# A banded self-attention stage: one product for values and softmax sums, reciprocals later, the output projection one unit later

## The reference, cut to the stage that changes

The program is a two-layer decoder: self-attention, cross-attention and a mixture of experts, twice. Only the first self-attention is touched. It has 8 batches of 256 rows, 256 features, 16 heads of 16, and a band: a query sees the keys at most 64 rows away.

## Times and profile before

| | us |
|---|---|
| median of three runs | 1502.38 (1500.22 to 1503.75) |
| the profiled execution | 1504.03 |
| its span in the profile | 1502.4 |
| PE busy in it | 1433.9 (95%) |
| DVE, ACT, POOL busy | 748.7, 619.1, 490.5 |

### The profile page before, as it was taken

One profiled execution on the slowest core, in us unless ns is written; L12 is line 12 of the kernel. 1 busy time (PEld: TensorE's weight loads), 2 busy tenths in 40 slices (PEclk: granted clock), 3 DMA queues, 4 the chain that ended last, 5 costly groups with the idle time before them and its releaser, 6 DMA issues. The chain is left out here.

```text
span 1502.4 us, 34667 instructions
## 1 busy us (share of the span) xinstructions
PE 1433.9 (95%) x11880; PEld 1159.7 (77%) x11881; DVE 748.7 (50%) x2160; ACT 619.1 (41%) x1711; POOL 490.5 (33%) x758
## 2 busy tenths in 40 slices
PE   7999998988999999999999999999899899999998
PEld 5676766767899999976777777777666579999997
DVE  6666757887433333344444444444278862222222
ACT  2433346653222222235445444545366533333332
POOL 3545442444322122223233233333224452222222
PEclk9999999999999999999999999999999999999999
DMA  9920000152243434120000000000001522533332
GB/s 316 333 69 2 2 2 9 45 176 62 50 119 67 144 71 114 32 64 1 0 1 1 1 1 1 1 1 0 1 16 44 174 78 40 149 93 94 94 90 34
DMA packets 79666, 97.46 MB, mean 65 GB/s; under 512 B 10523, under 2 KB 72579, under 8 KB 79555
## 3 DMA queue, kind: packets, MB, share of 16 engines
q1 hardware_dynamic: 64643, 77.58, 16.4%
q0 software_dynamic: 13680, 17.19, 6.6%
q10 hardware_dynamic: 1232, 1.18, 0.2%
HBM read 57.51 MB, written 39.59 MB: 65 GB/s over the span
## 5 line engine op out<-in xcount | busy, mean ns | idle before, releaser
L1741 POOL TENSOR_TENSOR L1a_prob<-L1a_prob,L1a_rtot 128x1024 f32<-128x1024 f32 x64 | 121.1, 1892 | 275.8 <-DVE L1a_rtot L1614 275.8
L2270 PEld LDWEIGHTS L0x_ps<-L0f_rows_t,L0f_w_up 128*128 128x128 f32 x1584 | 183.7, 193 | 10.4 <-issue 9.0
L2270 PE MATMUL L0x_ps<-L0f_rows_t,L0f_w_up 128*128 128x128 f32 x1584 | 185.8, 277 | 5.6 <-issue 4.8
L2346 ACT ACTIVATE L1f_hid<-L1x_ps,L1f_b_up 128x128 f32<-128x128 f32 x296 | 92.4, 363 | 163.0 <-PE L1x_ps L2270 159.7
L2270 PEld LDWEIGHTS L1x_ps<-L1f_rows_t,L1f_w_up 128*128 128x128 f32 x1184 | 139.5, 194 | 3.4 <-issue 1.6
L2270 PE MATMUL L1x_ps<-L1f_rows_t,L1f_w_up 128*128 128x128 f32 x1184 | 140.4, 277 | 0.6 <-ACT L1f_rows_t L2330 0.6
L2279 PE MATMUL L1x_ps<-L1f_w_down,L1f_hid 128*128 128x256 f32 x592 | 134.1, 380 | 1.9 <-issue 1.9
L2214 POOL TENSOR_TENSOR turn<-eps 128x1 f32<-128x1 f32 x74 | 13.6, 184 | 372.3 <-DVE wv L2448 367.7
L1683 ACT ACTIVATE L1a_prob<-L1a_ps_s,L1a_nmax 128x256 f32<-128x256 f32 x256 | 118.2, 473 | 38.1 <-DVE L1a_nmax L1609 38.1
L2279 PEld LDWEIGHTS L1x_ps<-L1f_w_down,L1f_hid 128*128 128x128 f32 x592 | 109.6, 190 | 15.5 <-issue 2.1
L1245 POOL TENSOR_SCALAR_AFFINE_SELECT L0a_prob<-L0a_prob 128x128 f32<-128x128 f32 (+1 forms) x256 | 79.8, 353 | 104.3 <-ACT L0a_prob L1199 104.3
(11 more groups left out here) (486 smaller groups left out, 2812.5 us busy)
## 6 DMA issues: line engine op xcount, KB each, us to landing
expert_table<-zero SPq DMA_DIRECT2D x1, 16640.0 KB, 68.5
L0f_w_up<-in_w_dram SPq DMA_DIRECT2D x8, 1408.0 KB, 6.8
L1f_w_up<-in_w_dram SPq DMA_DIRECT2D x8, 1024.0 KB
L1f_w_down<-in_w_dram SPq DMA_DIRECT2D x8, 1024.0 KB
L0f_w_down<-in_w_dram SPq DMA_DIRECT2D x8, 768.0 KB, 8.7
L1f_rows<-expert_table SPq DMA_DIRECT2D x35, 130.0 KB
L0f_rows<-expert_table SPq DMA_DIRECT2D x32, 130.0 KB
sums<-X SPq DMA_DIRECT2D x8, 256.0 KB
```

Source lines behind the costliest of these rows:

```text
L1741: eng.tensor_tensor(v, v, r.unsqueeze(2).to_broadcast([P, 2 * QT_N, S]), ALU.mult).then_inc(norm_done, 1)
L2270: ins = eng.matmul(ps_h[c][:, o:o + P], w_up[par][:, t, w0:w0 + P], rows_t[:, t, :], start=(t == 0), stop=(t == DT - 1))
L2346: ins = eng.activation(hid[:, c, k * P:(k + 1) * P], ps_h[c][:, k * P:(k + 1) * P], ACT.Gelu, bias=b_up[par][:, 2 * c + k:2 * c + k + 1])
```

```diff
-    MID = [[], [(1, "k")], [(-1, "o")], []]
+    MID = [[], [(1, "k")], [], [(-1, "o")]]
...
+        def weights_of(i, t, head):
+            columns = v_s[i][:, t, :, :].rearrange("p h n -> p (h n)")
+            return columns[:, 2 * DH * head - head % 2:2 * DH * (head + 1) - head % 2]
+        def direct(u):
+            return u >= units - 2
...
                 def sums(b, c):
-                    eng.wait_ge(values_done, 2 * (b * 2 + c + 1))
-                    eng.reciprocal(rsum[:, :], ps_o[:, S:2 * S]).then_inc(rsum_done, 1)
+                    n = b * 2 + c
+                    if n:
+                        eng.wait_ge(o_out, n)
+                    if direct(2 * n):
+                        eng.wait_ge(values_done, 2 * (n + 1))
+                        eng.reciprocal(rsum[:, :], ps_o[:, S:2 * S]).then_inc(rsum_done, 1)
+                    else:
+                        eng.wait_ge(sums_moved, 32 * (n + 1))
+                        eng.reciprocal(rsum[:, :], summed_t[:, :]).then_inc(rsum_done, 1)
...
-                    whole = part(u - 2)[:2] if v == 1 and u > 1 else None
-                    if whole:
-                        sums(*whole)
+                    whole = part(u - 4)[:2] if v == 0 and u >= UNITS else part(u - 2)[:2] if u == units - 1 else None
...
                     shift(u)
-                    if whole:
-                        out(*whole)
                     if u + 1 < units:
                         for r in range(GROUPS):
                             maximum(u + 1, r)
-                    for e in of(MID, u):
+                    if whole:
+                        sums(*whole)
+                        out(*whole)
+                    if u == units - 6:
+                        eng.wait_ge(values_done, u - 1)
+                        eng.memset(v_s[(B - 1) % 2][:, :, HEADS // 2:HEADS, :], 0.0).then_inc(cleared, 1)
+                    for e in of(MID, u) + of(END, u):
                         take(*e)
...
+                def gather(n):
+                    eng.wait_ge(values_done, 2 * (n + 1))
+                    if n:
+                        eng.wait_ge(sums_moved, 32 * n)
+                        eng.wait_ge(values_moved, 32 * n)
+                    eng.activation(both[:, :, :], ps_o[:, :].rearrange("p (w s) -> p w s", w=2), ACT.Copy).then_inc(copied, 1)
+                def move(n):
+                    eng.wait_ge(copied, n + 1)
+                    if n:
+                        eng.wait_ge(o_out, n)
+                    for w in range(2):
+                        eng.dma_start(summed_t[w::2, :], both[1 - w::2, w, :]).then_inc(sums_moved, 16)
+                    for w in range(2):
+                        eng.dma_start(valued_t[w::2, :], both[w::2, w, :]).then_inc(values_moved, 16)
...
+                    if u % 2 == 1 and u > 1:
+                        move(u // 2 - 1)
                     for r in range(GROUPS):
                         exponential(u, r)
+                    if u % 2 == 0 and u:
+                        gather(u // 2 - 1)
...
-                            eng.wait_ge(o_out, u // 2)
-                    for summed in range(2):
+                            eng.wait_ge(copied, u // 2)
+                    for summed in range(2 if direct(u) else 1):
```

More of the change, by code:

```diff
@@ L1005, in attention_banded @@
         rsum, o_t = sb("rsum", [P, S]), sb("o_t", [P, 2, S])
+        both, summed_t, valued_t = sb("both", [P, 2, S]), sb("summed", [P, S]), sb("valued", [P, S])
         built, cleared, tops_cleared = sem("built"), sem("cleared"), sem("tops_cleared")
@@ L1044, in wait_free @@
                 eng.wait_ge(exp_done, u * GROUPS + r + 1)
-        def odd_even(v):
-            return v.rearrange("p (a two) (half d) -> p a (two half) d", two=2, half=2)[:, :, 0::3, :]
+        def weights_of(i, t, head):
[3 more added lines that the diff above has]
+            return u >= units - 2
         with nc.Block() as block:
@@ L1064, in _ @@
                     eng.wait_ge(built, 4 * v + 3)
-                    eng.memset(ones[:, v, v * DH:(v + 1) * DH], 1.0).then_inc(built, 1)
+                    eng.memset(ones[:, v, v::2], 1.0).then_inc(built, 1)
                 eng.memset(none[:, :], 0.0).then_inc(built, 1)
@@ L1095, in take @@
                         ins.then_inc(out_vector, 1)
-                    elif e == "o":
+                    if e == "o":
                         eng.wait_ge(projected, b + 1)
@@ L1116, in sums @@
                 def sums(b, c):
-                    eng.wait_ge(values_done, 2 * (b * 2 + c + 1))
-                    eng.reciprocal(rsum[:, :], ps_o[:, S:2 * S]).then_inc(rsum_done, 1)
+                    n = b * 2 + c
[7 more added lines that the diff above has]
+                        eng.reciprocal(rsum[:, :], summed_t[:, :]).then_inc(rsum_done, 1)
                 def out(b, c):
-                    eng.wait_ge(rsum_done, b * 2 + c + 1)
+                    n = b * 2 + c
+                    eng.wait_ge(rsum_done, n + 1)
                     if c == 0 and b:
                         eng.wait_ge(projected, b)
-                    eng.tensor_tensor(o_t[:, c, :], ps_o[:, 0:S], rsum[:, :], ALU.mult).then_inc(o_out, 1)
+                    if not direct(2 * n):
+                        eng.wait_ge(values_moved, 32 * (n + 1))
+                    eng.tensor_tensor(o_t[:, c, :], ps_o[:, 0:S] if direct(2 * n) else valued_t[:, :], rsum[:, :], ALU.mult).then_inc(o_out, 1)
                 norm(0, 0)
@@ L1130, in _ @@
                 for i in range(2):
-                    eng.memset(v_s[i][:, :, :, :], 0.0).then_inc(cleared, 1)
+                    eng.memset(v_s[i][:, :, :, :], 1.0).then_inc(cleared, 1)
                 norm(1, 0)
@@ L1188, in take @@
                     else:
-                        eng.wait_ge(cleared, 2)
+                        eng.wait_ge(cleared, 3 if b == B - 1 else 2)
                         for t in range(KT):
-                            ins = eng.activation(odd_even(v_s[b % 2][:, t, :, :]), src[:, t, :].rearrange("p (a two d) -> p a two d", two=2, d=DH),
-                                                 ACT.Copy)
+                            ins = eng.activation(v_s[b % 2][:, t, :, 0::2], src[:, t, :].rearrange("p (h d) -> p h d", d=DH), ACT.Copy)
                     ins.then_inc(out_scalar, 1)
@@ L1341, in values @@
                         if u:
-                            eng.wait_ge(o_out, u // 2)
-                    for summed in range(2):
+                            eng.wait_ge(copied, u // 2)
+                    for summed in range(2 if direct(u) else 1):
                         for t in range(KT):
                             for r in range(GROUPS):
-                                o = summed * S + first_key[t]
-                                lhs = ones[:, v, :] if summed else v_s[b % 2][:, t, c * 8 + 2 * r + v, :]
-                                ins = eng.matmul(ps_o[rows(r), o:o + W], lhs, prob[u % 2][:, r, t, :], start=(v == 0 and not summed and t == 0),
-                                                 stop=(v == 1 and t == KT - 1), skip_group_check=True)
+                                o = (summed if direct(u) else v) * S + first_key[t]
+                                lhs = ones[:, v, :] if summed else weights_of(b % 2, t, c * 8 + 2 * r + v)
+                                ins = eng.matmul(ps_o[rows(r), o:o + W], lhs, prob[u % 2][:, r, t, :],
+                                                 start=(t == 0 and (v == 0 and not summed if direct(u) else True)),
+                                                 stop=(t == KT - 1 and (v == 1 or not direct(u))), skip_group_check=True)
                     ins.then_inc(values_done, 1)
@@ L2719, with in_turn @@
     down0[:, 0:full + GATED_TAIL] = i["L0_ffn_W3"].transpose(0, 2, 1)
+    def in_turn(w):
+        return w.reshape(-1, 2, 16, *w.shape[1:]).swapaxes(1, 2).reshape(w.shape)
     laid = {
```

3 lines of the change are left out of this document (2 added, 1 removed).

## The result

The changed kernel has a median of 1494.43 us, against 1502.04 before: ratio 0.9943, interval 0.9921 to 0.9965, so 5 to 12 us faster. One of its four executions took 2434.47 us in a slower state, with a mean granted clock of 0.55; the ratio leaves it out, and the median of the other three is 1493.69. Its profiled execution has a span of 1492.0 us where before's had 1502.4.

A forecast was written before the change was run, and what follows sets the result against it. PE was taken as the bound, busy 170.17 of 173.00 us. First batch −1.7, six batches −9.4, last batch −0.9 and tail +3.2 sum to −8.8, so 1502.4 becomes 1493.6 us; range 1489 to 1499, 63%.

The forecast's parts named there:

- The six batches: Batches from the second on: products with ones removed, less new waits, give −1.57 us each, −9.4 in six.
- The floor: From `turned_scores` to the values of the same unit at least 4.40 us, set by exponentials and band selects.
- The first batch: No "o" there and unit 2 already at its minimum: of 2.68 us removed, −1.7 remains.
- the issues end about 1.5 before it is needed: Ahead of unit 4, ACT's DMA issues finish about 1.5 us before ACT is needed.
- ACT's margin: Ahead of unit 2's exponentials, ACT has 0.65 us to spare with four DMA issues of 0.49 each.
- Rival 2: ACT's issues at 0.9 delay unit 2, about 1501 us (8%), or slow landings hold DVE, 1506 to 1515 (7%).
- The last batch: Unit 2 to unit 3 of the last batch: exponentials about 0.9 us late, gather costs 0.35, −0.9 in all.
- The tail: From `turned_scores` of unit 31 to the last "o": PE waits for the last move's chain, 3.2 us lost.
- Rival 1: More is gained, by a hidden tail wait or a better ring place for "o": 1487 to 1490 us, 8%.
- Rival 3: ACT cannot issue DMAs while SP's fill is queued, blocked to 79 us: 40 us lost, 1533 us, 14%.
- stays short even beside the big fill: Landing of ACT's DMAs to DVE, nearest row 2.1 us for 130 KB, remains short during SP's big fill.
- The barrier argument: Later stages begin behind a barrier, so the stage's −8.8 us carries through to the kernel's time.

The follow-up runs named there:

- half a band: Only one side of the band cut: on the changed kernel 1493.91 us, ratio 0.993; on the kernel before 1505.75 us, ratio 1.0001.
- "o" alone: The kernel before with only the projection "o" moved from unit 3 to unit 4 of a batch: 1514.5 us, ratio 1.006.
- The last run above: Changed kernel with DVE's copies and additions ahead of the reciprocal and the keys' projection moved to unit 3, run again: 1494.08 us, ratio 0.9911.

## Why the prediction came out right, step by step

**The six batches.** Forecast −1.57 each, measured 24.76 to 23.23, −1.53. Two terms inside were off and cancel. Both are 0.16. The wait that went with the move of "o" was taken as the 0.26 of the earlier trace rows; the step from unit 3 to unit 4 grew by 1.40 where "o" adds 1.82, so it was 0.42. The idle column counts only the time in which nothing runs; what the wait costs is seen in the starts. The other: from the values of unit 2 to the next `turned_scores` the forecast had 0.77, and it is 0.93, because the maxima free the bank for it only then. The run with half a band shows that second floor.

**The floor.** The 4.40 from the first batch, taken for every unit, held to 0.01 in unit 2 and unit 4 of each quiet batch. Of 2.68 removed a batch the forecast lost 1.11 again and the kernel 1.15; with the product issued twice the batch got 1.48 longer.

**The first batch.** −1.22 instead of −1.7. Unit 2 lost 0.16 to the maxima, as everywhere. In unit 4 the exponentials came 0.25 late behind the first issues, which beside the fill ended at 40.27:

```profile
38.51 1.76 ACTq L1238 DMA_DIRECT2D L0a_valued<-L0a_both  x2
40.38 1.64 ACT L1219 ACTIVATE L0a_prob<-L0a_ps 128x384 f32<-128x384 f32 x4 [2.50 <-PE L0a_ps L1373]
```

The step that failed is that ahead of unit 4 "the issues end about 1.5 before it is needed": in this one unit the last two issues took 0.88 each, not 0.49. Ahead of unit 4 of the quiet batches it held (108.48 against 110.06). The −0.45 ahead of this batch was not forecast, and nothing in the change accounts for it: before had 29.34, and its variants 28.90 ("o" alone) and 29.98 (half a band), the changed kernel's 28.58 to 29.62. So some 0.5 of the 9.70 is not the change's.

**ACT's margin.** Forecast 0.65 with 0.49 an issue; measured 1.7 with 0.62. Both terms were off. The issue is dearer (a DMA of 64 rows of 1 KB, 0.47 to 0.62). But the working put the issues behind the copies of the queries, and they run beside them: 94.18 against 95.49, 1.3 us won. Rival 2's rule, that it decides at 0.65 an issue, was therefore too near; it would decide near 1.0. Doubled issues crossed it at once, so the mechanism of the rival is real and only its distance was wrong.

**The last batch.** This is the largest miss, −2.14 instead of −1.23 (with the 0.35 for the gather, −0.9), with the same cause. The forecast let the exponentials of unit 30 come 0.9 late behind four issues, and put 0.35 on the gather. The issues ran beside ACT's other work, the exponentials came 0.92 after `turned_scores` at 190.52 (at 191.44, 0.36 behind the last issue, which ended at 191.08), and the wait for `ct` grew from 0.84 to 0.91 only.

**The tail.** Forecast +3.2, measured +3.41. The number is right and the account of it only in part. PE before, then the changed kernel:

```profile
211.47 0.93 PE L1331 MATMUL L0a_ps<-L0a_q_m,L0a_k_m 32*128 32x192 f32 x16 [0.51 <-DVE L0a_q_m L1114]
```

```profile
198.66 1.97 PE L1330 MATMUL L0a_ps<-wo,L0a_o_t 128*128 128x256 f32 x8 [0.81 <-DVE L0a_o_t L1142]
200.55 0.93 PE L1373 MATMUL L0a_ps<-L0a_q_m,L0a_k_m 32*128 32x192 f32 x16
...
205.83 1.13 PE L276 MATMUL L0a_ps<-wo,L0x_bv_wide 128*128 128x256 f32 x4 [0.95 <-DVE X L1108]
```

The chain over the last move is the one described. The last values start at 206.89, which is 11.21 after `turned_scores` of unit 31 at 195.68, forecast 11.0. The reciprocal started 5.65 behind `turned_scores`, not 7.15, and then the product waited 1.49 for the outputs' move, which the forecast had let arrive with the sums: of its two DMAs one landed in 1.9 us and one in 3.9.

But the chain is not what the 3.41 is made of. `turned_scores` of unit 31 to that of unit 32 was 211.47 − 208.79 = 2.68 and is 200.55 − 195.68 = 4.87, 2.19 longer, because the moved "o" of batch 7 now stands between them, with a wait of 0.81 for DVE. From there to the last values it was 5.12 and is 6.34, and only these 1.22 are the chain. Where the last move landed in time or the addition stood ahead of it, the last values came at 9.99 and the tail still lost 2.18. So the forecast's "if it were hidden this would be 0" is wrong: it counted what the moved "o" saves in unit 3 of the last batch and not what it adds in unit 4. The number was met by luck: the reciprocal started 1.5 earlier than forecast, and with a landing of 2 us for the outputs too, the chain would not have shown, as in the kernel with the product issued twice; one landing of 3.9 brought it back. Why that one was late isn't shown. In the repeat of the changed kernel (landing 3.2) the tail lost 2.81. In the whole sum the misses are −0.45 ahead of the first batch, +0.5 in it, −0.25 in the six, −0.9 in the last and +0.2 in the tail, so some of its nearness is that they cancel.

**The rivals.** Rival 1's cause, a hidden tail, didn't come. Rival 3, ACT blocked while SP's fill is in the queues, is refuted by two rows of SP's and ACT's queues in the changed kernel:

```profile
21.95 58.22 SPq L2694 DMA_DIRECT2D wr<-in_wr_dram  x1
...
37.31 0.53 ACTq L1236 DMA_DIRECT2D L0a_summed<-L0a_both  x1
```

SP's issue was held from 21.95 to 80.2; ACT's, in the middle of it, took 0.53, and the longest of all during the fill 1.6. So in this trace ACT's queue is not held with SP's, and what the prediction held possible here, that the two block each other's commands, did not come. The Trainium skill ("DMA: Bandwidth & Descriptors", section "Queues, rings and completion order") gives SP and ACT one ring each on the same 16 DMA engines; the trace agrees with the second part, the shared engines: landings took 5.0 to 6.2 us beside the fill, and 1.9 in the median behind it. So the landing that "stays short even beside the big fill" was three times as long there; it cost nothing, as DVE needs the tiles later. Of its signs of being wrong one came, once: DVE was idle 2.49 for a DMA before L1133, in the tail, where its own sum had it.

**The carry to the end.** The barrier argument held for the profiled execution (−9.67 at the next stage, −10.4 at the end) and for the medians within their interval (−7.6, or −8.35 with the median of 1493.69, with −5 to −12). But it is less exact than these two numbers look: between them the lead was 13.5 (at the expert products behind 396 us of before) and 11.8 (at 720), while both kernels run the same code. The last run above is a warning about it too: the next stage can return several us by its clock.

## What to carry to other kernels

A product that is removed from the bounding engine is worth its time only down to the next chain's floor, and a place in the program where that floor already shows (here the first batch, without "o") gives its size to 0.01. Read waits on a pipelined engine from start to start: the idle column gave 0.26 for 0.42. When a freed engine waits in one unit and is full in the next, move work into the wait (here "k"), and when a move leaves it idle for some us, count the granted clock behind the idle time, not the wait alone. Where an entry moves across the end of a loop, count it on both sides: the move of "o" saved its time in one unit of the last batch and added 2.19 in the next.

## What the runs showed of the hardware

- **The clock.** After 4.58 us without a product TensorE had a granted clock of 0.58 over 88 to 94 us, "o" from 1.89 to 3.75. The same wait filled with 36 records of identity products kept it at 1.00 and gave 2.4 us a batch back.
- **Issues beside copies.** ACT's DMA issues start while its earlier ACTIVATEs run (by 1.3 us here), though later ACTIVATEs wait for them.
- **Two readers of SBUF.** Before, the product read its first operand from PSUM and took 0.42 in all 16 places. In the changed kernel L1142 has both operands in SBUF and runs beside POOL's selects: 0.67 or 0.68 in 11 of 15 places, 0.61 in one and 0.43 in three. POOL's eight took 2.65 to 2.80 there, and 2.46 in units 2 and 4. One place of either kind:

```profile
93.22 0.68 DVE L1142 TENSOR_TENSOR L0a_o_t<-L0a_valued,L0a_rsum 128x256 f32<-128x256 f32 x1
```

```profile
92.97 2.65 POOL L1287 TENSOR_SCALAR_AFFINE_SELECT L0a_prob<-L0a_prob 128x128 f32<-128x128 f32 x8 [1.50 <-ACT L0a_prob L1219]
```

```profile
187.12 0.43 DVE L1142 TENSOR_TENSOR L0a_o_t<-L0a_valued,L0a_rsum 128x256 f32<-128x256 f32 x1
```

  Beside the last one POOL's row is 2.73. With "o" in the third unit the same product ran at 89.85, when POOL had nothing, in 0.42. The Trainium skill ("SBUF — State Buffer", section "SBUF: two separate sides") says that a DVE instruction with two SBUF inputs and a GpSimd instruction that reads SBUF share a pair of ports as an exclusive lock, which the one that starts first has for its whole instruction. The trace agrees where single selects can be told apart: at 93.21 a select started just ahead of the product, which took 0.68; at 46.66 the product started first and took 0.43, and the select behind it, at 46.76, took 0.59 where others of its form take 0.40; at 187.14, behind the product at 187.12, one took 0.67. It cost nothing here, as neither stands in units 2 and 4, which set the floor. But the operand that moved from PSUM to SBUF made the step dearer, where the prediction had taken 0.35 for it.
